# Norms of queries and keys by logarithm and exponential, their multiplication on GpSimd, and a new place for ScalarE's first squares

## The chip, the cores and the metric

One core of a Trainium2 chip runs the whole program. The metric is the device time of one execution in microseconds, as the median of several runs. Lower is better. The engines are TensorE (PE; PEld is its weight load), VectorE (DVE), ScalarE (ACT), GpSimd (POOL) and SyncE (SP), which issues DMAs. Each takes its own list of instructions in order, and they wait for each other by semaphores.

## What is computed

The reference is a sequence of four attention blocks and four feed-forward blocks on x of shape 8 x 512 x 128. The change lies in one of them, the local transformer with six layers, 16 heads of 64 and windows of 32 tokens. Its attention, cut to what matters here:

```
qkv = x @ Wqkv                        # 128 -> 3 x 1024
q, k, v = split(qkv), heads of 64
q = q / max(norm(q), 1e-12) * q_scale
k = k / max(norm(k), 1e-12) * k_scale
q = q * cos * scale + rotate_half(q) * sin * scale
k = k * cos / scale + rotate_half(k) * sin / scale
sim = q k^T * 8, in blocks of 32 queries by 64 keys, masked
out = softmax(sim) v
x = x + out @ Wo, then x + feed-forward with GELU, for each of six layers
```

The norm is a number per token and head. It can be multiplied in after the rotation, since the rotation is linear.

## The kernel before

The phase in question is `local_transformer_phase`. It takes the tokens of one sequence (512) as four tiles of 128, and so 6 layers x 8 sequences x 4 = 192 tiles; the text calls the four of a sequence tiles 0 to 3 (k % 4 in the code). Each engine runs one loop over k from -2 to 199 with the same stages in it, so that tile k is in its attention while the queries and keys of tile k + 1 are being finished and tile k + 2 is being projected. The order on each engine is the order of the calls in its loop; nothing else sorts them.

In iteration k, TensorE makes the scores of tile k (`make_scores`, L1205 and L1212), the values of k + 1 (`project_v`), the queries of k + 2 (`project_qk(.., 0)`, L1184 to L1186), turns the attention output of k - 1 (`turn_out`, L1273), makes the keys of k + 2 (`project_qk(.., 1)`), turns the probabilities of k (`turn_probs`, L1249), turns queries and then keys of k + 1 (`turn_qk`, L1262, eight transposes each), weighs the values of k in two halves (`weigh_values`, L1288) with the output projection of k - 1 between them (`project_out`, L1300), and does one step of the feed-forward block of an earlier sequence: `ffn_a` (L1338) in tile 0, `ffn_out` (L1343) and `ffn_turn` (L1316) in tile 1, `ffn_back` (L1323) in tile 2, `ffn_gate` (L1332) in tile 3.

Two waits of TensorE matter. The keys of tile k + 1 are turned into banks 4 and 5, which hold the projected queries of k + 2 until VectorE has read them; so `turn_qk(m, 1)` waits for `products_ready` of tile m + 1. And `project_out` writes bank 2, from which ScalarE copies the turned queries; so it waits for `qkt_copied`.

VectorE, in iteration k: `centre` (row maximum and subtraction of the scores, L1585 and L1588), `normalise` of queries and keys of k + 1 (L1595, rotated values times inverse norm), `products` of k + 2 (L1605, the projected values times cosines into `rot`, times sines into `sines`, for queries and then keys), `sum_squares` (L1610), in tile 2 `ffn_shift` (L1643), `divide` (L1616 and L1620), the second `sum_squares`, `add_output`, the second `divide`. In tile 1 the statistics of the feed-forward block come last (L1632 to L1639); they give `var_ready`.

`products(m, a)` waits for `squared` of the same tile, since ScalarE squares the same banks first. ScalarE, in iteration k: `copy_v` of k + 1 (L1413), `exponentials` of k (L1406), `square(k + 2, 0)` (L1418, queries), `copy_out` of k - 1 (L1435), `square(k + 2, 1)` (keys), `copy_probs` of k (L1423), `copy_qk` of k + 1 for queries and keys (L1430), and then the feed-forward step: `copy_turned` in tile 1, `ffn_normalise` (L1450) and `scale_norm` (L1457) in tile 2, `gelus` (L1464) in tile 3, with a table load before and after (L1460 and L1465). `ffn_normalise` waits for VectorE's shift, and `ffn_back` on TensorE for `ffn_normalise`.

GpSimd, in iteration k: in tile 2 `invert_deviation` (L1538, a power), `rotate` of k + 2 (L1526, four additions of 128x512 in place in `rot`), in tile 1 the low halves of the next sequence's tokens (L1516 and L1517), then `invert_norms` of k + 2 for queries and keys (L1532 guards the sum of squares from below, L1534 raises it to the power -1/2).

## Time and profile before

| | us |
|---|---|
| median of three runs | 4828.77 |
| lowest and highest run | 4828.52, 4838.41 |
| profiled execution, its own time | 4834.84 |
| its span | 4832.9 |
| TensorE busy (share) | 4224.5 (87%) |
| VectorE busy | 3624.7 (75%) |
| GpSimd busy | 2849.5 (59%) |
| ScalarE busy | 2545.3 (53%) |

The busy shares are an average over all phases of the program. A group row gives the busy time of one line, the mean of one instruction in ns, and then the idle time of its engine right before it with what ended that. A timeline row gives start and duration in us; where several equal instructions were merged, "x8" says how many, and the duration is that of all. In brackets stands the idle time of the engine before it and who ended it. Matmuls overlap, so starts are compared with starts.

### The profile page before, as it was taken

Reading aid. Unit: us, or ns where it says so; the run is one execution under the profiler, and the core shown is the slowest. Engines: PE = TensorE matmul, PEld = TensorE weight load, DVE = VectorE, ACT = ScalarE, POOL = GpSimd, SP = SyncE. Lnnn points to the kernel's source line nnn. Section 1 sums busy time; section 2 is a strip of 40 time slices with the busy share of each in tenths; the row PEclk is TensorE's granted clock in tenths of the full one; section 3 lists DMA queues with packets and bytes.
Section 4 is the critical chain, followed back from the end, with each engine's and each line's share of the span. In section 5 each row is a group of like instructions: output and inputs, shape, how many; then the busy total and the mean of one; then the engine's idle time right before and its main releaser. Section 6 shows DMA issues by size and latency. Waiting matters only on the chain. (4 is left out here: it accounts for less than half of the span.)

```text
span 4832.9 us, 167342 instructions
## 1 busy us (share of the span) xinstructions
PE 4224.5 (87%) x70890; PEld 3379.5 (70%) x70890; DVE 3624.7 (75%) x5894; ACT 2545.3 (53%) x3896; POOL 2849.5 (59%) x2141
## 2 busy tenths in 40 slices
PE   6997899999999999999999999999997749658667
PEld 5885677777777777777777777777775439548447
DVE  4445888888888888888888888888885564564554
ACT  2232456655566556565556565566654317546435
POOL 2223777777777777777777777777772037516025
PEclk9776999999999999999999999999998869868878
DMA  0001222232222322222222222222221021222022
GB/s 25 0 0 39 75 63 63 69 79 69 63 70 62 85 62 70 64 80 67 67 67 80 68 63 70 63 68 67 67 66 37 0 59 50 68 61 61 7 63 74
DMA packets 214198, 281.51 MB, mean 58 GB/s; under 512 B 58878, under 2 KB 103716, under 8 KB 212740
## 3 DMA queue, kind: packets, MB, share of 16 engines
q1 hardware_dynamic: 203972, 251.85, 20.1%
q0 software_dynamic: 9536, 19.55, 1.4%
q8 instruction: 545, 8.93, 0.8%
q14 instruction: 145, 1.19, 0.1%
HBM read 54.88 MB, written 18.28 MB: 15 GB/s over the span
## 5 line engine op out<-in xcount | busy, mean ns | idle before, releaser
L1526 POOL TENSOR_TENSOR local_rot<-local_rot,local_sines 128x512 f32<-128x512 f32 x768 | 955.2, 1278 | 825.1 <-DVE local_sines L1605 825.1
L1534 POOL TENSOR_TENSOR local_inv_norm<-local_norm2c,minus_half 128x16 f32<-128x16 f32 x384 | 1126.9, 2935 | 32.0
L1413 ACT COPY local_v_tile<-local_bank 128x1024 f32<-128x1024 f32 x192 | 195.0, 1016 | 713.0 <-PE local_bank L1186 702.6
L1184 PE MATMUL local_bank<-local_wqkv_hi,local_ys_hi 128*128 128x512 f32 x1152 | 491.3, 426 | 23.6 <-POOL local_ys_lo L1517 10.4
L1262 PE MATMUL local_bank<-ident,local_normed 128*128 128x128 f32 x3072 | 405.4, 275 | 91.0 <-DVE local_sines L1605 80.6
L1595 DVE TENSOR_TENSOR local_normed<-local_rot,local_inv_norm 128x1024 f32<-128x1024 f32 x384 | 455.3, 1218 | 32.9 <-issue 26.4
L1605 DVE TENSOR_TENSOR local_rot<-local_bank,local_table 128x1024 f32<-128x1024 f32 x384 | 467.7, 1218 | 7.0 <-issue 7.0
L1605 DVE TENSOR_TENSOR local_sines<-local_bank,local_table 128x1024 f32<-128x1024 f32 x384 | 467.3, 1217 | 0.0
L1610 DVE TENSOR_REDUCE local_norm<-local_squares 128x16 f32<-128x1024 f32 x384 | 464.7, 1211 | 0.0
L1186 PE MATMUL local_bank<-local_wqkv_hi,local_ys_lo 128*128 128x512 f32 x1152 | 453.8, 394 | 0.0
L1185 PE MATMUL local_bank<-local_wqkv_lo,local_ys_hi 128*128 128x512 f32 x1152 | 453.3, 394 | 0.0
L1585 DVE TENSOR_REDUCE local_top<-local_bank 128x16 f32<-128x1024 f32 x192 | 234.8, 1223 | 272.4 <-PE local_bank L1212 272.4
L1262 PEld LDWEIGHTS local_bank<-ident,local_normed 128*128 128x128 f32 x3072 | 339.9, 142 | 132.4 <-issue 120.5
L1300 PE MATMUL local_bank<-local_att_t,local_wo 128*128 128x128 f32 x3072 | 396.7, 283 | 1.6 <-ACT local_att_t L1435 1.3
L1418 ACT ACTIVATE local_squares<-local_bank 128x1024 f32<-128x1024 f32 x384 | 393.0, 1024 | 9.2 <-PE local_bank L1186 6.2
L1300 PEld LDWEIGHTS local_bank<-local_att_t,local_wo 128*128 128x128 f32 x3072 | 359.9, 193 | 20.0 <-ACT local_att_t L1435 1.5
L1288 PE MATMUL local_bank<-local_vals,local_probs_t 64*32 64x65 f32 x24576 | 336.7, 225 | 5.3 <-issue 3.0
L1212 PEld LDWEIGHTS local_bank<-local_k_t,local_q_t 64*32 64x32 f32 x24576 | 256.2, 105 | 104.7 <-issue 104.5
L1288 PEld LDWEIGHTS local_bank<-local_vals,local_probs_t 64*32 64x32 f32 x24576 | 270.3, 106 | 64.0 <-issue 39.6
L1212 PE MATMUL local_bank<-local_k_t,local_q_t 64*32 64x64 f32 x24576 | 289.8, 226 | 20.4 <-issue 20.4
L1620 DVE TENSOR_TENSOR local_att<-local_bank,local_inv_sum 128x512 f32<-128x512 f32 x384 | 265.5, 691 | 13.2
L1184 PEld LDWEIGHTS local_bank<-local_wqkv_hi,local_ys_hi 128*128 128x128 f32 x1152 | 217.6, 189 | 77.9 <-issue 25.7
...
## 6 DMA issues: line engine op xcount, KB each, us to landing
...
```

Source lines behind the costliest of these rows:

```text
L1184: nc.tensor.matmul(out, hi, wqkv_hi[:, d0:d1], start=True, stop=False)
L1185: nc.tensor.matmul(out, hi, wqkv_lo[:, d0:d1], start=False, stop=False)
L1186: return nc.tensor.matmul(out, lo, wqkv_hi[:, d0:d1], start=False, stop=True)
L1212: last = nc.tensor.matmul(bank[b * BLOCK:(b + 1) * BLOCK, SCORES[odd], c * WIN:(c + 1) * WIN], q_t[rows, c, b * BLOCK:(b + 1) * BLOCK], k_ ...
L1262: last = nc.tensor.transpose(bank[:, QK_TURN[a][j // 4], j % 4 * P:(j % 4 + 1) * P], normed[:, (8 * a + j) * P:(8 * a + j + 1) * P], g.ide ...
L1288: last = nc.tensor.matmul(bank[b * BLOCK:(b + 1) * BLOCK, WEIGHED[i][odd], j * (HD + 1):(j + 1) * (HD + 1)], probs_t[rows, c, b * BLOCK:(b ...
L1300: last = nc.tensor.matmul(bank[:, WO_BANK, 0:P], wo[:, c, :], att_t[:, c, :], start=(c == 0), stop=(c == CH - 1))
L1526: last = nc.gpsimd.tensor_tensor(of_heads(rot, a)[:, :, to], of_heads(rot, a)[:, :, to], of_heads(sines, a)[:, :, of], ALU.add)
L1534: nc.gpsimd.tensor_tensor(inv_norm[:, cols], norm2c[:, cols], g.minus_half[:, cols], ALU.pow).then_inc(q["inv_norms_ready"], 1)
L1595: nc.vector.tensor_tensor(of_heads(normed, a), of_heads(rot, a), inv_norm[:, a * HEADS:(a + 1) * HEADS].unsqueeze(2).to_broadcast([P, HEAD ...
L1605: last = nc.vector.tensor_tensor(of_heads(out, a), src, table[:, m % TILES, row, :].unsqueeze(1).to_broadcast([P, HEADS, HD]), ALU.mult)
L1610: nc.vector.tensor_reduce(norm2[:, cols], of_heads(squares, a), AX, ALU.add).then_inc(q["norms_ready"], 1)
```

## The change

Four things change, all in the local phase.

- The multiplication by the inverse norm (`normalise`) goes from VectorE to GpSimd. `rotate` now writes its sums into `normed`, and `normalise` multiplies `normed` in place. Since `normed` is what TensorE turns, `rotate` of a tile waits for `qk_turned` of the tile before, and `normalise` waits for the inverse norms.
- GpSimd's power is gone. It guards all 32 sums of squares in one instruction (`guard_norms`), and ScalarE makes the inverse norms as exp(-0.5 ln n) in two activations of 128x32, at the head of its iteration k for tile k + 1 (`invert_norms`).
- `square(k + 2, 0)` stands ahead of `exponentials(k)` instead of behind it.
- Both functions, and the exponential of the softmax, come from one table set that is loaded by name, once ahead of the loop and once after each sequence's gelus, there in place of a tiny exponential that had caused the load.

VectorE's `products(m, a)` now waits for `rotated` of tile m - 1, and `sum_squares` for `norms_guarded` of it.

```diff
+                def invert_norms(m):
+                    act.wait_ge(q["norms_guarded"], tile("norms_guarded", m))
+                    nc.scalar.activation(log_norm[:], norm2c[:], ACT.Ln).then_inc(q["logs_ready"], 1)
+                    act.wait_ge(q["logs_ready"], tile("logs_ready", m))
+                    act.wait_ge(q["qk_normed"], tile("qk_normed", m - 1))
+                    nc.scalar.activation(inv_norm[:], log_norm[:], ACT.Exp, scale=-0.5).then_inc(q["inv_norms_ready"], 1)
...
-                    nc.scalar.activation(table_pick[:, 2:3], table_pick[:, 0:1], ACT.Exp)
-
+                    nc.scalar.preload_act_table_set("natural_log_exp_and_others")
+
+                nc.scalar.preload_act_table_set("natural_log_exp_and_others")
...
                     if is_tile(k + 1):
+                        invert_norms(k + 1)
                         copy_v(k + 1)
+                    if is_tile(k + 2):
+                        square(k + 2, 0)
                     if is_tile(k):
                         exponentials(k)
-                    if is_tile(k + 2):
-                        square(k + 2, 0)
...
                     pool.wait_ge(q["products_ready"], tile("products_ready", m, a + 1))
+                    pool.wait_ge(q["qk_turned"], tile("qk_turned", m - 1, a + 1))
...
-                        last = nc.gpsimd.tensor_tensor(of_heads(rot, a)[:, :, to], of_heads(rot, a)[:, :, to], of_heads(sines, a)[:, :, of], ALU.add)
+                        last = nc.gpsimd.tensor_tensor(of_heads(normed, a)[:, :, to], of_heads(rot, a)[:, :, to], of_heads(sines, a)[:, :, of], ALU.add)
...
-                def invert_norms(m, a):
...
-                    nc.gpsimd.tensor_tensor(inv_norm[:, cols], norm2c[:, cols], g.minus_half[:, cols], ALU.pow).then_inc(q["inv_norms_ready"], 1)
+                def guard_norms(m):
+                    pool.wait_ge(q["norms_ready"], tile("norms_ready", m))
+                    nc.gpsimd.tensor_scalar(norm2c[:], norm2[:], 1e-24, None, ALU.max).then_inc(q["norms_guarded"], 1)
+
+                def normalise(m, a):
+                    pool.wait_ge(q["rotated"], tile("rotated", m, a + 1))
+                    pool.wait_ge(q["inv_norms_ready"], tile("inv_norms_ready", m))
+                    nc.gpsimd.tensor_tensor(of_heads(normed, a), of_heads(normed, a), inv_norm[:, a * HEADS:(a + 1) * HEADS].unsqueeze(2).to_broadcast([P, HEADS, HD]),
+                                            ALU.mult).then_inc(q["qk_normed"], 1)
...
+                    if is_tile(k + 1):
+                        normalise(k + 1, 0)
+                        normalise(k + 1, 1)
                     if is_tile(k + 2):
                         rotate(k + 2, 0)
                         rotate(k + 2, 1)
...
-                        invert_norms(k + 2, 0)
-                        invert_norms(k + 2, 1)
+                        guard_norms(k + 2)
...
-                    dve.wait_ge(q["qk_normed"], tile("qk_normed", m - 1, a + 1))
+                    dve.wait_ge(q["rotated"], tile("rotated", m - 1, a + 1))
...
-                    if is_tile(k + 1):
-                        normalise(k + 1, 0)
-                        normalise(k + 1, 1)
```

ScalarE's list in a tile 2, before, from the values to the keys:

```order
L1413 COPY local_v_tile<-local_bank 128x16x64
L1406 ACTIVATE local_scores<-local_scores 128x1024
L1418 ACTIVATE local_squares<-local_bank 128x1024
L1435 COPY local_att_t<-local_bank 128x1024
L1418 ACTIVATE local_squares<-local_bank 128x1024
L1423 COPY local_probs_t<-local_bank 128x1024
L1430 COPY local_q_t<-local_bank 128x1024
L1430 COPY local_k_t<-local_bank 128x8x128
```

The same place in the changed kernel (its line numbers are higher):

```order
L1436 ACTIVATE local_log_norm<-local_norm2c 128x32
L1439 ACTIVATE local_inv_norm<-local_log_norm 128x32
L1415 COPY local_v_tile<-local_bank 128x16x64
L1420 ACTIVATE local_squares<-local_bank 128x1024
L1408 ACTIVATE local_scores<-local_scores 128x1024
L1444 COPY local_att_t<-local_bank 128x1024
L1420 ACTIVATE local_squares<-local_bank 128x1024
L1425 COPY local_probs_t<-local_bank 128x1024
L1432 COPY local_q_t<-local_bank 128x1024
L1432 COPY local_k_t<-local_bank 128x8x128
```

The first squares and the exponentials have changed places, and the two small activations stand at the head.

GpSimd's list around a tile 2, before: the end of tile 1 (from the low halves on), the power for the deviation, and rotation and norms of tile 2:

```order
L1516 TENSOR_TENSOR local_ys_lo<-XH,local_ys_hi 64x512
L1517 TENSOR_TENSOR local_ys_lo<-XH,local_ys_hi 64x512
L1532 TENSOR_SCALAR local_norm2c<-local_norm 128x16
L1534 TENSOR_TENSOR local_inv_norm<-local_norm2c,minus_half 128x16
L1532 TENSOR_SCALAR local_norm2c<-local_norm 128x16
L1534 TENSOR_TENSOR local_inv_norm<-local_norm2c,minus_half 128x16
L1538 TENSOR_TENSOR local_rstd<-local_var_eps,minus_half 128x4
L1526 TENSOR_TENSOR local_rot<-local_rot,local_sines 128x16x32 x4
```

The same place in the changed kernel:

```order
L1527 TENSOR_TENSOR local_ys_lo<-XH,local_ys_hi 64x512
L1528 TENSOR_TENSOR local_ys_lo<-XH,local_ys_hi 64x512
L1543 TENSOR_SCALAR local_norm2c<-local_norm 128x32
L1553 TENSOR_TENSOR local_rstd<-local_var_eps,minus_half 128x4
L1548 TENSOR_TENSOR local_normed<-local_normed,local_inv_norm 128x1024 x2
L1538 TENSOR_TENSOR local_normed<-local_rot,local_sines 128x16x32 x4
```

The four instructions for the norms have become one, and the two multiplications stand between the deviation and the rotation of the tile after.

## Rows read from the trace of the kernel before

**Rows 1.** windows of the phase: stretch, length, busy time (count) by engine
```profile
510.00:3680.00 3170.00, 3008.07 (x63005) 2357.83 (x62989) 2764.74 (x3546) 1885.73 (x2278) 2299.29 (x1654) 1.00 0.27 69
```

**Rows 2.** waits of the whole span: who waited for whom, total us, times, longest
```profile
PE local_bank L1262 <- DVE local_sines L1605: 80.6, 185, 4.5
```

**Rows 3.** timeline of TensorE, tile 0: start, us, engine, line, operation, count [idle before]
```profile
2025.42 0.39 PE L1186 MATMUL local_bank<-local_wqkv_hi,local_ys_lo 128*128 128x512 f32 x1
...
2027.91 1.04 PE L1249 MATMUL local_bank<-ident,local_scores 128*128 128x128 f32 x8
2028.78 1.04 PE L1262 MATMUL local_bank<-ident,local_normed 128*128 128x128 f32 x8
2030.04 1.06 PE L1262 MATMUL local_bank<-ident,local_normed 128*128 128x128 f32 x8 [0.22 <-DVE local_sines L1605]
2031.04 0.86 PE L1288 MATMUL local_bank<-local_vals,local_probs_t 64*32 64x65 f32 x64
2031.83 2.05 PE L1300 MATMUL local_bank<-local_att_t,local_wo 128*128 128x128 f32 x16
```

**Rows 4.** timeline of ScalarE, the same tile
```profile
2025.39 1.06 ACT L1406 ACTIVATE local_scores<-local_scores 128x1024 f32<-128x1024 f32 x1
2026.36 1.01 ACT L1418 ACTIVATE local_squares<-local_bank 128x1024 f32<-128x1024 f32 x1
2027.27 1.00 ACT L1435 COPY local_att_t<-local_bank 128x1024 f32<-128x1024 f32 x1
2028.15 1.04 ACT L1418 ACTIVATE local_squares<-local_bank 128x1024 f32<-128x1024 f32 x1
2029.08 1.01 ACT L1423 COPY local_probs_t<-local_bank 128x1024 f32<-128x1024 f32 x1
2029.96 1.04 ACT L1430 COPY local_q_t<-local_bank 128x1024 f32<-128x1024 f32 x1
```

**Rows 5.** timeline of TensorE, tile 2 (the third) of the sequence before
```profile
1996.38 1.04 PE L1262 MATMUL local_bank<-ident,local_normed 128*128 128x128 f32 x8
1998.40 1.07 PE L1262 MATMUL local_bank<-ident,local_normed 128*128 128x128 f32 x8 [0.98 <-DVE local_sines L1605]
...
2003.92 0.63 PE L1323 MATMUL local_bank<-ident,local_y_hat 128*128 128x128 f32 x4 [0.89 <-ACT local_y_hat L1450]
```

**Rows 6.** timeline of VectorE, the same tile 2
```profile
1990.53 0.17 DVE L1639 TENSOR_SCALAR local_var_eps<-local_mean_var 128x4 f32<-128x4 f32 x1
...
1998.17 1.22 DVE L1605 TENSOR_TENSOR local_rot<-local_bank,local_table 128x1024 f32<-128x1024 f32 x1
...
2001.55 0.54 DVE L1643 SCALAR_TENSOR_TENSOR local_shift<-local_mean_var,local_rstd 128x4 f32<-128x4 f32 x1
```

**Rows 7.** timeline of ScalarE, the same tile 2
```profile
2002.12 1.65 ACT L1450 ACTIVATE local_y_hat<-local_y_tok,local_shift,local_rstd 128x128 f32<-128x128 f32 x4 [1.61 <-DVE local_shift L1643]
```

**Rows 8.** GpSimd's groups by form: line, names, shapes, count, busy us, mean ns
```profile
L1534 POOL TENSOR_TENSOR local_inv_norm<-local_norm2c,minus_half 128x16 f32<-128x16 f32 x384 | 1126.9, 2935 | 32.0
L1526 POOL TENSOR_TENSOR local_rot<-local_rot,local_sines 128x512 f32<-128x512 f32 x768 | 955.2, 1278 | 825.1 <-DVE local_sines L1605 825.1
...
L388 POOL TENSOR_SCALAR moe_row_of<-moe_at_col,moe_row_id 128x1136 bf16<-128x1136 bf16 x4 | 19.5, 4882 | 0.0
...
L387 POOL TENSOR_TENSOR moe_row_of<-moe_at_col,moe_row_id 128x1136 bf16<-128x1136 bf16 x4 | 12.9, 3235 | 38.4 <-DVE moe_at_col L520 38.4
...
L2023 POOL TENSOR_TENSOR delta_wkbd<-delta_wkb,delta_e_dec 128x512 f32<-128x512 f32 x8 | 8.4, 1046 | 0.0
```

**Rows 9.** ScalarE's groups by form, a very small one
```profile
L1977 ACT ACTIVATE delta_ln_u<-delta_e_u 128x4 f32<-128x4 f32 x8 | 1.6, 205 | 0.1
```

**Rows 10.** timeline of ScalarE, end of the tile 3 ahead of that tile 0
```profile
2021.73 1.28 ACT L1465 ACT_TABLE_LOAD   x1
```

**Rows 11.** timeline of GpSimd, filling of the phase
```profile
478.10 0.27 POOL L1532 TENSOR_SCALAR local_norm2c<-local_norm 128x16 f32<-128x16 f32 x1
```

**Rows 12.** timeline of TensorE, filling of the phase
```profile
489.23 1.94 PE L1262 MATMUL local_bank<-ident,local_normed 128*128 128x128 f32 x8 [4.50 <-DVE local_sines L1605]
```

21 lines of the change are left out of this document (7 added, 14 removed).

## The prediction

> **What bounds the kernel now.** I first cut the span by phases. The windows view shows that the local transformer phase takes 3,170 of 4,833 us from its second tile on, and that TensorE is busy for 3,008 of them at a granted clock of 1.00 (its upper level, 2.4 GHz), while VectorE has 2,765, GpSimd 2,299 and ScalarE 1,886 [rows 1]. So at most 162 us are to be had from waits of TensorE in this phase; relief of any other engine is worth only what it takes from them. The phase handles 192 tiles, four to a sequence; I call them tiles 0 to 3. The waits view then names the largest hole with a cause in another engine: before the turning of queries and keys (L1262) TensorE waits for VectorE's products of the next tile, 80.6 us in 185 times [rows 2]. The timelines say how they arise. In an ordinary tile the turning of queries starts at 2028.78 and that of keys at 2030.04, 1.26 us later, though its eight transposes need only what the turning of the probabilities takes ahead of it (2027.91 to 2028.78, 0.87 us) [rows 3]. The gap is therefore 0.39 us from start to start. In tile 2 it is 2.02 instead of 0.87 [rows 5], and there comes a second hole, 0.89 us in which TensorE waits for ScalarE's feed-forward rows at 2003.92 [rows 5].
>
> **The part taken from VectorE.** The two normalising multiplications (L1595), which stand ahead of the products, leave VectorE in each tile. That alone moves nothing: the products also wait for the squares, which ScalarE makes. Hence the new place of the first squares. I work through an ordinary tile by its rows. The last matmul of the query projection ends at 2025.42 + 0.39 = 2025.81 [rows 3], and ScalarE follows TensorE by 0.04, so the squares start at 2025.85. ScalarE's steps, from start to start, are 0.91 for squares, 0.97 for the exponentials, 0.88 for the copy of the turned output (2027.27 to 2028.15), 0.93 for the second squares and 0.88 for the probabilities [rows 4]. In the new order the squares end at 2026.9 (2027.4 before). The query products, freed of the normalising, take 2.3 us from 2026.9 and end at 2029.2, ahead of 2029.65, when TensorE could start on the keys. The wait for them goes.
>
> **What is late next.** The exponentials now start at 2026.76 and end at 2027.82; TensorE wants them at 2027.91 [rows 3], so this costs at most 0.1 if the signal takes long. The rest of ScalarE's chain: copy at 2027.73, second squares at 2028.61, probabilities at 2029.54 and ready at 2030.55, queries at 2030.42 and ready at 2031.46. The weighing (L1288) wants the probabilities; without its old delay it would start at 2031.04 - 0.39 = 2030.65. The output projection (L1300) writes the bank that the copy of the queries reads, so it can start at 2031.46 plus a signal. Signals from ScalarE to TensorE took 0.15 at the end of tile 2 (2002.12 + 1.65 = 2003.77, then 2003.92) [rows 5, 7]; the shortest that I grant is 0.05. The projection started at 2031.83 [rows 3]; it now starts at 2031.51 to 2031.61, a gain of 0.22 to 0.32. With the other delays of this chain (a late exponential moves nothing but the probabilities) I take 0.24. ScalarE has become as tight as TensorE: that is why I don't book the full 0.39. Tiles 0, 1 and 3 are 144: 144 x 0.24 = 34.6 us, with ends of 0 (each signal 0.15 slower than I think) and 144 x 0.39 = 56.
>
> **Tile 2.** It lies 32.40 us ahead of the ordinary one (1996.38 against 2028.78) [rows 3, 5], so its first squares start at 1993.45, the second at 1993.45 + 0.91 + 0.97 + 0.88 = 1996.21 and end at 1997.25. The key products start then; before, they started at 1998.17 [rows 6]. From there to the shift (L1643) it is two products and a sum of squares, as before: 2001.55 - 1998.17 = 3.38 [rows 6]. So the shift comes at 2000.67, 0.87 us sooner, ScalarE's rows (L1450) and TensorE's turning back with it. TensorE itself would be there yet sooner, so it still waits; what counts is the 0.87. In 48 sequences: 41.8 us, with ends of 30 (the shift gains two thirds) and 48 x 1.15 = 55 (the whole hole of the keys).
>
> **The new steps on ScalarE.** Two activations of 128x32 a tile. The smallest of this kind took 205 ns [rows 9]; with the wait between them I take 0.6 us. They stand ahead of the copy of the values, where ScalarE is idle: the copy waits for TensorE. In tile 0 this is narrow: the table load after the last gelu ends at 2021.73 + 1.28 = 2023.01 [rows 10], the norms are there at 2023.65, and the copy is due some 0.9 us ahead of the exponentials of 2025.39 [rows 4], at 2024.5. The code names one table set for logarithm and exponential, and the order of the changed kernel has no load between them; it has one more in all, ahead of the first weight split, where ScalarE sits idle anyway. I cost all this at nothing; its cover in tile 0 is 0.8 us.
>
> **The new steps on GpSimd.** Two multiplications of 128x1024 by a spread operand. The nearest row is L2023, the same operation on 128x512: 1046 ns, so 2.1 us each; by the additions of rotate it is 2 x 1278 = 2.56 [rows 8], and by the bfloat16 rows at the most 3235 x 1024 / 1136 = 2.9 [rows 8]. I take 2.1. GpSimd gives up two powers of 2.9 us a tile [rows 8] and gets some 4.2, so it isn't fuller. The question is when it is done. In tile 0 it starts at 2023.65 and ends the keys at 2027.9; TensorE wants them at 2029.65. In tile 2 it first waits for the variance (1990.53 + 0.17) [rows 6], makes its power of about 1.0 us, starts at 1991.8 and ends at 1996.0; wanted are the queries at 1996.38 and the keys at 1997.25. Both fit, with 1.7 and 1.2 us over. Tile 3 has its norms behind the feed-forward rows of ScalarE, by my working 7.1 us ahead of the keys' time, and tile 1 has yet more.
> The new wait of rotate for the turned queries and keys (it writes the buffer that TensorE reads) has the guard of the norms queued behind it: rotate starts at about 2029.9, as now, and the guard comes at 2035, long before the next tile's logarithm.
> On what GpSimd costs the page GPSIMD Engine Reference of the Trainium skill (3.1, Elementwise) speaks against the change: about 2.6 cycles an element with two inputs, twice VectorE's time. By that the price would be 2.2 us, an estimate from the page; the sum stays as it is, since this fits into the 3.0 that tile 0 leaves.
>
> **The fill.** For tile 0 of the phase the chain is bare. The guard ends at 478.37 [rows 11]; then came two powers and the normalising, and the keys were turned at 489.23 after a wait of 4.50 [rows 12]. Now: norms at 479.05, ScalarE's copy and squares to 481.1, query products to 483.4, GpSimd's keys at 483.3, keys turned at 483.5. That is 5.7 us once.
>
> **Sum.** 34.6 + 41.8 + 5.7 = 82.1 us. The profiled execution took 4834.84 us with a span of 4832.9; the median of the runs is 4828.77, 6 us lower, and the steps are the same in it. I take the sum from the median: 4746.7, so **4747 us**. Layer changes (five) are priced like their neighbours, though VectorE is the bound there and could give a little more.
>
> **Rivals.**
> *ScalarE eats the ordinary tiles.* Exponentials and probabilities come each 0.9 us later, and TensorE waits at L1249 or L1288 for what it saved at L1262. For it: the margins worked out above are 0.1 us. Against it: every step is from this trace. Tiles 0, 1, 3 then give nothing: 4828.8 - 47.5 = 4781.
> *TensorE alone bounds.* The chain of ScalarE is a little faster than I add up: 0.39 in each of 144 tiles, 0.87 in 48, 5.7 and some 6 at layer changes: 4828.8 - 110 = 4719.
> *GpSimd becomes late, slower than before.* Gelus, table load, logarithm, exponential and two slow multiplications are one chain in tile 0; variance, power and the same two in tile 2. At p us each, the keys are late by 2p - 6.0 in tile 0 (2023.65 + 2p against 2029.65) and by 2p - 5.5 in tile 2. A sequence gains 1.7 us, so it turns at 4p - 11.5 = 1.7, p = 3.3. The nearest row on that side is the two-step GpSimd operation at 4.88 us for 1136 elements, 4.4 for 1024 [rows 8]. At p = 4, with 0.9 in tile 3, it is 5.4 us a sequence on top of 4747: about 5005. Against it stand two rows of 2.1 and 2.6.
> *Nothing comes of it.* Another wait of the same size stands at the same place, say the keys' bank still waits for products: 4829.
>
> **How the numbers follow.** My forecast has a chance of 0.70 (4730 to 4765), the eaten tiles 0.11, TensorE alone 0.08, GpSimd late 0.07, nothing 0.04. A range of 4712 to 4790 takes the first three. About 0.2% is what a measurement of this kernel can tell from no change: faster 0.89, same 0.04, slower 0.07.
>
> **What would show it.** Right: the line "PE L1262 waits for VectorE's sines" gone or under 10 us in all; ordinary tiles of about 16.2 us from L1205 to L1205 instead of 16.45; tile 2 about 15.1; the shift row 0.9 sooner after the turned queries; GpSimd's multiplication at 2.0 to 2.6 us; ScalarE and GpSimd named nowhere before L1262. Wrong: waits of TensorE for the exponentials (L1249) or the probabilities (L1288) of over 0.2 us a tile; waits at L1262 for GpSimd; table loads beside the pairs around the gelus; a VectorE that runs slower while GpSimd multiplies.

## The result and the profile after

The changed kernel takes **4804.4 us** (median of four runs, 4800.65 to 4813.37) against 4829.24 us for the kernel before in the same set: a ratio of 0.9947, 95% interval 0.9928 to 0.9966. It is faster, by 25 us. Forecast were 82 us and a range of 4712 to 4790, so the time lies outside the range. In microseconds at 4829 the interval means 17 to 35 us less. The profiled execution took 4813.37 us with a span of 4811.3.

The windows view of the phase, changed kernel (stretch, length, busy time and count of PE, PEld, VectorE, ScalarE, GpSimd, then granted clock, DMA share, GB/s); it answers [rows 1]:

```profile
510.00:3680.00 3170.00, 3033.77 (x63121) 2367.06 (x63119) 2395.78 (x3172) 1948.63 (x2617) 1868.62 (x1462) 0.99 0.26 68
```

VectorE lost 369 us of work and GpSimd 431. TensorE gained only 26 in an equal stretch of time, and its clock is no longer 1.00 on the mean.

TensorE's waits inside the phase, from 500 to 3640 (who waited for whom, total us, times, longest), first before, then after:

```profile
PE local_bank L1262 <- DVE local_sines L1605: 75.9, 183, 3.7
PE local_bank L1323 <- ACT local_y_hat L1450: 39.0, 44, 0.9
PE local_bank L1212 <- issue: 19.5, 14, 1.9
PE local_bank L1184 <- issue: 7.0, 5, 1.4
...
PE local_bank L1288 <- issue: 3.0, 6, 0.9
```

```profile
PE local_bank L1325 <- ACT local_y_hat L1459: 47.7, 46, 1.5
PE local_bank L1214 <- issue: 32.3, 24, 1.9
PE local_bank L1290 <- issue: 23.9, 59, 1.7
PE local_bank L1186 <- issue: 15.4, 5, 3.1
```

The wait of [rows 2] at the turned queries and keys is gone: L1264 (L1262 before) is not in the list. But 76 us of waits went and 25 came off the time. "issue" means that TensorE stood still and the profile names no other engine. I call these the unnamed gaps; the entries shown grew from 29.5 to 71.6 us (19.5 + 7.0 + 3.0, then 32.3 + 23.9 + 15.4).

TensorE in tile 0 of a sequence, changed kernel; it answers [rows 3]:

```profile
2012.94 1.05 PE L1251 MATMUL local_bank<-ident,local_scores 128*128 128x128 f32 x8
2013.89 1.94 PE L1264 MATMUL local_bank<-ident,local_normed 128*128 128x128 f32 x16
2015.76 0.86 PE L1290 MATMUL local_bank<-local_vals,local_probs_t 64*32 64x65 f32 x64
2016.63 2.02 PE L1302 MATMUL local_bank<-local_att_t,local_wo 128*128 128x128 f32 x16
```

All sixteen transposes are one row now. From the probabilities' transposes to the output projection it is 3.69 us, 3.92 before (2031.83 - 2027.91, [rows 3]): the forecast's step for ordinary tiles, 0.24, is there to 0.01.

The same for tile 2, with VectorE's shift; it answers [rows 5, 6]:

```profile
1981.88 1.94 PE L1264 MATMUL local_bank<-ident,local_normed 128*128 128x128 f32 x16
...
1986.59 0.34 PE L1290 MATMUL local_bank<-local_vals,local_probs_t 64*32 64x65 f32 x14
1987.34 0.73 PE L1290 MATMUL local_bank<-local_vals,local_probs_t 64*32 64x65 f32 x50 [0.41 <-issue]
1988.69 0.63 PE L1325 MATMUL local_bank<-ident,local_y_hat 128*128 128x128 f32 x4 [0.62 <-ACT local_y_hat L1459]
```

```profile
1986.10 0.76 DVE L1654 SCALAR_TENSOR_TENSOR local_shift<-local_mean_var,local_rstd 128x4 f32<-128x4 f32 x1
```

The shift comes 4.22 us after the first turned queries, 5.17 before; but it takes 0.76 instead of 0.54, and the rows of the feed-forward are turned back 6.81 us after them instead of 7.54. So 0.73 is left of the 0.87.

What was added cost about what the forecast said: GpSimd's multiplication from the page's groups (mean 1926 ns), ScalarE's two activations from the views of their lines (least, median, largest ns):

```profile
L1548 POOL TENSOR_TENSOR local_normed<-local_normed,local_inv_norm 128x1024 f32<-128x1024 f32 x384 | 731.6, 1926 | 326.3 <-ACT local_inv_norm L1439 326.3
```

```profile
L1436 ACT ACTIVATE local_log_norm<-local_norm2c x192: 217/229/245, 479.4 to 3641.5; 128x32 f32<-128x32 f32 x192
L1439 ACT ACTIVATE local_inv_norm<-local_log_norm x192: 229/229/232, 479.6 to 3641.8; 128x32 f32<-128x32 f32 x192
```

**Where the time went.** I took TensorE's timeline of 46 sequences (all but the first and the last) and measured each stretch from its first start to the first start of the next kind. This is the ledger, with means of one sequence (four tiles) in us:

| stretch | before | after | difference |
|---|---|---|---|
| turned queries and keys (L1264) | 9.70 | 7.47 | -2.23 |
| turned probabilities (L1251) | 3.60 | 3.72 | +0.12 |
| first half of the weighing (L1290) | 3.17 | 3.50 | +0.33 |
| output projection (L1302) | 7.97 | 7.84 | -0.13 |
| second half, with tile 2's wait for ScalarE's rows | 4.25 | 5.13 | +0.88 |
| scores (L1214) | 6.21 | 6.52 | +0.31 |
| projections and turned output (L1186, L1275) | 20.88 | 21.35 | +0.47 |
| feed-forward products and band | 10.99 | 10.99 | 0 |
| sum | 66.77 | 66.51 | -0.26 |

46 x 0.26 = 12 us. The first scores came 5.2 us sooner (492.27 before, 487.06 after), and the remaining sequences and the end hold the last 4 of the 21.6 us between the two spans. Of 2.23 us that a sequence gained, 1.97 came back in other places. Some of that the forecast had taken off already (it booked 0.24 of 0.39 in an ordinary tile, and 0.87 of 1.15 in tile 2). The first half of the weighing is such a case: it isn't slower. In the changed kernel the output projection starts 0.14 us after the end of ScalarE's copy of the turned queries in all four kinds of tile (medians), in the kernel before 0.7 to 1.4 us after it; so TensorE now waits there for ScalarE, as the forecast had it, in a pause too short for the wait list. The experiments are about the other places: the projections (five layer changes), the second half of the weighing (the shift, and gaps), the scores (gaps).

### The profile page after: what moved, and what is told of

It reads as the page before. It is cut to its first block and busy times, and to the rows that moved or that the text cites. A ratio compares the mean times of both kernels' runs of the same rounds, so it can differ in the third digit from the quotient of the medians.

```text
span 4811.3 us, 167679 instructions
## 1 busy us (share of the span) xinstructions
PE 4235.1 (88%) x70890; PEld 3379.2 (70%) x70890; DVE 3249.3 (68%) x5510; ACT 2605.4 (54%) x4233; POOL 2417.1 (50%) x1949
## 3 DMA queue, kind: packets, MB, share of 16 engines
q8 instruction: 545, 8.93, 0.8%
## 5 line engine op out<-in xcount | busy, mean ns | idle before, releaser
L1538 POOL TENSOR_TENSOR local_normed<-local_rot,local_sines 128x512 f32<-128x512 f32 x768 | 953.5, 1276 | 788.6 <-PE local_bank L1264 784.0
L1548 POOL TENSOR_TENSOR local_normed<-local_normed,local_inv_norm 128x1024 f32<-128x1024 f32 x384 | 731.6, 1926 | 326.3 <-ACT local_inv_norm L1439 326.3
L1186 PE MATMUL local_bank<-local_wqkv_hi,local_ys_hi 128*128 128x512 f32 x1152 | 496.2, 431 | 31.6 <-issue 15.4
L1615 DVE TENSOR_TENSOR local_sines<-local_bank,local_table 128x1024 f32<-128x1024 f32 x384 | 466.5, 1215 | 0.0
L1302 PE MATMUL local_bank<-local_att_t,local_wo 128*128 128x128 f32 x3072 | 390.4, 280 | 4.4 <-ACT local_att_t L1444 1.2
L1302 PEld LDWEIGHTS local_bank<-local_att_t,local_wo 128*128 128x128 f32 x3072 | 358.7, 192 | 30.3 <-issue 12.9
L1264 PE MATMUL local_bank<-ident,local_normed 128*128 128x128 f32 x3072 | 373.6, 275 | 4.7 <-POOL local_normed L1548 4.1
L1290 PE MATMUL local_bank<-local_vals,local_probs_t 64*32 64x65 f32 x24576 | 348.8, 225 | 26.4 <-issue 23.9
L1264 PEld LDWEIGHTS local_bank<-ident,local_normed 128*128 128x128 f32 x3072 | 333.8, 142 | 23.9 <-POOL local_normed L1548 5.4
L1290 PEld LDWEIGHTS local_bank<-local_vals,local_probs_t 64*32 64x32 f32 x24576 | 273.7, 105 | 94.0 <-issue 69.7
L1214 PEld LDWEIGHTS local_bank<-local_k_t,local_q_t 64*32 64x32 f32 x24576 | 256.2, 105 | 118.9 <-issue 118.9
L1214 PE MATMUL local_bank<-local_k_t,local_q_t 64*32 64x64 f32 x24576 | 291.4, 225 | 33.3 <-issue 33.1
L1186 PEld LDWEIGHTS local_bank<-local_wqkv_hi,local_ys_hi 128*128 128x128 f32 x1152 | 220.2, 191 | 86.0 <-issue 33.9
L1188 PEld LDWEIGHTS local_bank<-local_wqkv_hi,local_ys_lo 128*128 128x128 f32 x1152 | 219.9, 191 | 50.9
```

Of the source, the lines that this page charges most:

```text
L1186: nc.tensor.matmul(out, hi, wqkv_hi[:, d0:d1], start=True, stop=False)
L1188: return nc.tensor.matmul(out, lo, wqkv_hi[:, d0:d1], start=False, stop=True)
L1214: last = nc.tensor.matmul(bank[b * BLOCK:(b + 1) * BLOCK, SCORES[odd], c * WIN:(c + 1) * WIN], q_t[rows, c, b * BLOCK:(b + 1) * BLOCK], k_ ...
L1264: last = nc.tensor.transpose(bank[:, QK_TURN[a][j // 4], j % 4 * P:(j % 4 + 1) * P], normed[:, (8 * a + j) * P:(8 * a + j + 1) * P], g.ide ...
L1290: last = nc.tensor.matmul(bank[b * BLOCK:(b + 1) * BLOCK, WEIGHED[i][odd], j * (HD + 1):(j + 1) * (HD + 1)], probs_t[rows, c, b * BLOCK:(b ...
L1302: last = nc.tensor.matmul(bank[:, WO_BANK, 0:P], wo[:, c, :], att_t[:, c, :], start=(c == 0), stop=(c == CH - 1))
```

## The experiments

Two theories stood at the start. **LOCK**: VectorE's operations with two inputs in SBUF and GpSimd's now longer and otherwise placed operations slow each other; that is the loss at the layer changes and at the shift. **FETCH**: the "issue" gaps are TensorE waiting for its own instructions, and they grow since the waits that used to hide this are gone. The rival to both was that ScalarE's new order (the squares ahead of the exponentials) moved the losses there. The edits are to the changed kernel unless another is named. The runs were made in sets, each with the kernel before in it, whose median lay between 4828 and 4836 us. Where a difference between two kernels of different sets is small, I give it twice, by the medians and by the ratios to the kernel before (in us at 4829).

### The layer changes

The three engines around the layer change at 2042, changed kernel:

```profile
2042.83 5.76 DVE L1596 TENSOR_TENSOR local_wqkv_lo<-local_stage,local_wqkv_hi 128x1024 fp32r<-128x1024 f32 x2
```

```profile
2042.64 4.87 POOL L1548 TENSOR_TENSOR local_normed<-local_normed,local_inv_norm 128x1024 f32<-128x1024 f32 x2
```

```profile
2045.85 0.76 PE L1186 MATMUL local_bank<-local_wqkv_hi,local_ys_hi 128*128 128x512 f32 x1 [3.09 <-issue]
```

VectorE splits two thirds of the new layer's weights while GpSimd multiplies. TensorE needs the first split: it ended at 2045.75, and TensorE went on at 2045.85. So this hole is a wait for VectorE, though the profile calls it "issue", and it belongs to LOCK, not to FETCH. Least, median and largest ns of the split, before (L1579) and after (L1596):

```profile
L1579 DVE TENSOR_TENSOR local_wqkv_lo<-local_stage,local_wqkv_hi x18: 1211/1224/1237, 460.1 to 3145.8; 128x1024 fp32r<-128x1024 f32 x18
```

```profile
L1596 DVE TENSOR_TENSOR local_wqkv_lo<-local_stage,local_wqkv_hi x18: 1221/2918/2921, 461.4 to 3131.3; 128x1024 fp32r<-128x1024 f32 x18
```

**e1_yield**: GpSimd waits at the layer changes until both splits are made.

```diff
                     if is_tile(k + 1):
+                        if (k + 2) % PER_LAYER == 0 and k > 0 and is_tile(k + 2):
+                            pool.wait_ge(split_lo, 3 * ((k + 2) // PER_LAYER) + 2)
                         normalise(k + 1, 0)
```

> The changed kernel, but at a layer change GpSimd waits with its two multiplications until VectorE has split the first two parts of the new weights. In the changed kernel the two splits took 5.76 us beside the multiplications (2.35 before the change) and tile 2 of a layer change 21.2 us (19.1 before). Theory LOCK (a VectorE instruction with two inputs in SBUF and a GpSimd instruction hold each other up): splits back at 2.3 us, multiplications at 3.8 for two instead of 4.87, tile 2 of the five layer changes at about 18.4, so 5 x 2.9 = 14 us less than the changed kernel (about 4790), and no fall of the granted clock at the layer changes. Rival WEIGHTS LATE (the splits wait for the loaded weights or for ScalarE's cast, which now come later relative to TensorE): splits stay near 5.8 us, time as the changed kernel, 4804, or a little above.

Measured: 4792.03 us (six runs), ratio 0.991 (0.9894 to 0.9926), under the changed kernel by 12 us by the medians and by 18 by the ratios. By the ledger it is 17: 0.38 us in each of 46 sequences, nearly all of it in tile 2, where a layer change takes 17.8 us instead of 21.3. The split and TensorE's wait:

```profile
L1598 DVE TENSOR_TENSOR local_wqkv_lo<-local_stage,local_wqkv_hi x18: 1212/1215/1225, 460.9 to 3112.2; 128x1024 fp32r<-128x1024 f32 x18
```

```profile
PE local_bank L1186 <- issue: 6.9, 5, 1.4
```

Windows of 20 us over the same layer change, after and with the wait, which has it 6 us sooner (the third number from the right is the granted clock):

```profile
2040.00:2060.00 20.00, 14.68 (x313) 12.05 (x291) 19.18 (x29) 11.46 (x16) 10.94 (x7) 0.91 0.18 48
```

```profile
2034.00:2054.00 20.00, 15.85 (x456) 13.07 (x456) 17.65 (x32) 13.81 (x21) 10.43 (x9) 1.00 0.19 49
```

The splits are back at 1215 ns, the long hole of 3.1 us is 1.4 again, and the clock, which had fallen to the lower of its two levels (1.2 of 2.4 GHz) for 3.4 to 6.8 us behind each of these holes, stays at the upper one. The rival, that the splits wait for weights that come late, is out: it forecast splits of nearly 5.8 us for two. LOCK holds here: an operation with two SBUF inputs took 2.9 us instead of 1.2 beside GpSimd, and GpSimd's, which overlapped it, up to 2.88 us instead of 1.90. The Trainium skill says of the port pair that the two engines share ("SBUF — State Buffer", the section on the two separate sides) that it is an exclusive lock which the first of the two holds for its whole instruction. The trace agrees to about 0.1 us if they take turns by whole operations. At 2042.64 GpSimd's first multiplication starts; alone it takes 1.90, so it would end at 2044.54. The split that starts at 2042.83 ends at 2045.75, which is 2044.54 and its own 1.21. The second multiplication ends at 2047.51, against 2045.75 + 1.90 = 2047.65, and the second split at 2048.59, against 2047.51 + 1.21 = 2048.72. The products of VectorE, with one input in PSUM, took 1.22 us as before beside the same multiplications. **e4_multiply_on_vector**, further down, is a second test: with nothing of GpSimd's beside them the splits took 1.21 us and tile 2 of a layer change 19.1, as before the change.

### The shift

**e3_shift_on_gpsimd**: the four numbers per row of the shift are worked out by GpSimd right behind its power; VectorE only makes the negated mean, earlier.

```diff
+                    nc.vector.tensor_scalar(neg_mean[:], mean_var[:, :, 0], -1.0, None, ALU.mult)
...
-                    nc.vector.scalar_tensor_tensor(shift[:], mean_var[:, :, 0], -1.0, rstd[:], ALU.mult, ALU.mult).then_inc(q["shift_ready"], 1)
...
+                    pool.wait_ge(q["rstd_ready"], seq("rstd_ready", n))
+                    nc.gpsimd.tensor_tensor(shift[:], neg_mean[:], rstd[:], ALU.mult).then_inc(q["shift_ready"], 1)
```

> The changed kernel, but the shift (minus mean times inverse deviation) is made by GpSimd right after its power, 14 us ahead, instead of by VectorE behind the sums of squares, where it took 0.76 us (0.54 before the change, 0.16 when alone). Theory: the wait of TensorE before the turning back of the feed-forward rows (about 1.0 us in each of 46 tiles 2) hangs on VectorE's list; now ScalarE makes the rows right behind the copy of the keys, 1.5 us sooner, the wait goes, and tile 2 falls from 15.30 to about 14.4: 48 x 0.9 = 43 us less than the changed kernel, 4762, minus what stalls of TensorE without a cause in another engine take back. Rival SUPPLY (TensorE's own instruction stream stalls, a constant of the program): tile 2 falls but tile 3 grows by as much, 4795 to 4804.

Measured: 4757.84 us (4752.35 to 4760.55), ratio 0.9839 (0.9826 to 0.9851): 47 us less than the changed kernel by the medians, 52 by the ratios, and so about twice what the whole change gave. The shift's line and what TensorE then waits for:

```profile
L1556 POOL TENSOR_TENSOR local_shift<-local_neg_mean,local_rstd x48: 201/203/233, 575.9 to 3633.0; 128x4 f32<-128x4 f32 x48
```

```profile
PE local_bank L1215 <- issue: 36.2, 33, 2.2
PE local_bank L1291 <- issue: 21.1, 51, 1.2
```

The wait for ScalarE's rows, 47.7 us in 46 times, is gone. It never was a matter of arithmetic: 0.2 us of work stood in VectorE's list behind 3.4 us of products. Not all of the gain is the shift's. At a layer change GpSimd's multiplications now stand behind the shift, and start 0.1 us after the first split instead of 0.2 us ahead of it: it took 1.21 us in all five, only the second 2.92, and tile 2 of a layer change fell to 18.3 to 19.8 us.

**e10_before_shift** does the same to the kernel before, and nothing else.

> The kernel before, with one part of e3_shift_on_gpsimd alone: the shift is worked out by GpSimd behind its power, and VectorE makes the negated mean only; nothing else is changed. The wait of the feed-forward's copies for y_hat is 0.89 us in the 44 tiles that have it, 39 us. If that goes and TensorE starts its next products as before, 4790. If TensorE's own gaps ahead of the scores in the next tile take a third of it back, as in the changed kernel, 4803. If the wait goes to something else in the same place, 4829 stays.

Measured: 4819.33 us, ratio 0.9968 (0.9957 to 0.9978). That is 10 us by the medians of the two sets, 16 by the ratio, less than the 26 or 39 expected. Its two largest waits:

```profile
PE local_bank L1263 <- DVE local_sines L1608: 93.5, 184, 4.2
PE local_bank L1213 <- issue: 23.6, 27, 1.7
```

By the ledger, tile 2 fell from 16.33 to 15.44 us and tile 3 rose from 17.00 to 17.50; of that 0.50, 0.36 is a longer wait for VectorE's products and 0.17 the scores. In the kernel before VectorE was the next to be late, in the changed one it is not: by the ratios the shift is worth 16 us there and 52 here. So the change is worth more than its own time shows.

**e6_yield_shift** has both edits, e1's and e3's.

> The two edits of e1 and e3 together: GpSimd waits at layer changes until VectorE has split two parts of the weights, and GpSimd makes the shift. If the two are independent, the gains over the changed kernel add up: 48 us of e3 and 12 to 17 of e1, so about 4743 and a ratio of 0.981 to the kernel before. If the same slack is counted twice (a layer change's tile 2 has both), 4750.

Measured: 4741.09 us (4735.64 to 4755.75), ratio 0.9824 (0.9804 to 0.9843), the fastest of all by its median. The sum of the two gains had forecast about 4743, the rival (the same slack counted twice) 4750, a ratio of 0.984. The interval holds both, so the time doesn't decide between them. The trace shows what the wait adds to e3: both splits are at 1.21 to 1.23 us, and tile 2 of a layer change takes 16.6 to 16.8 us.

### Order and place of the work

**e2_old_order** puts the exponentials ahead of the first squares again, **e7_yield_shift_old** does that to e6.

```diff
-                    if is_tile(k + 2):
-                        square(k + 2, 0)
                     if is_tile(k):
                         exponentials(k)
+                    if is_tile(k + 2):
+                        square(k + 2, 0)
```

> The changed kernel with the exponentials again ahead of the first squares; all else stays. Theory of the prediction (the wait at L1262 goes because the squares are earlier): products of the queries end at about 29.65 instead of 29.2 on the clock of rows 3, just when TensorE wants them; ScalarE's chain of six starts 0.46 us earlier, since it need not idle for the query projection. Ordinary tiles 16.15 to 16.25 as in the changed kernel (16.20), time within 8 us of it. Rival ORDER CARRIES IT: the wait at L1262 comes back with some 0.25 us a tile, 144 x 0.25 = 36 us slower than the changed kernel, 4840.

> The kernel of e6_yield_shift (GpSimd waits at layer changes, shift on GpSimd) with the exponentials again ahead of the first squares on ScalarE. If the place of the squares is worth nothing here too, as in e2_old_order, the time is that of e6_yield_shift, 4741 us within 8. If the old order spares TensorE the short gaps behind the weighing products (4.7 us over 15 in e2_old_order against 23.9 over 59), up to 15 us less, 4726. If ScalarE now delays the value products or the queries' normalising, since the shift is gone and less time stands in tile 2, up to 10 us more.

Measured: 4807.1 us, ratio 0.9946 (0.9933 to 0.996), the same as the changed kernel; and 4755.84 us, ratio 0.9841 (0.9825 to 0.9857). That is 15 us over e6 by the medians, 8 by the ratios, and the two intervals overlap. The new place of the squares is worth nothing that is sure to show in the time. Three waits of e2:

```profile
PE local_bank L1214 <- issue: 30.3, 24, 1.9
...
PE local_bank L1264 <- DVE local_sines L1615: 10.8, 47, 0.5
...
PE local_bank L1290 <- issue: 4.7, 15, 1.5
```

A named wait of 10.8 us is back, and the unnamed one behind it fell from 23.9 to 4.7. This is an exchange, and e7 shows the same one (13.8 and 4.1). In undisturbed ordinary tiles e2 takes 16.31 us, against 16.45 before and 16.20 in the changed kernel. So 0.14 of the 0.25 come from freeing VectorE alone, without the new place of the squares, where the forecast said that this "alone moves nothing".

**e4_multiply_on_vector** gives the multiplications back to VectorE; logarithm, exponential and the new order stay.

```diff
-                    nc.gpsimd.tensor_tensor(of_heads(normed, a), of_heads(normed, a), inv_norm[:, a * HEADS:(a + 1) * HEADS].unsqueeze(2).to_broadcast([P, HEADS, HD]),
+                    nc.vector.tensor_tensor(of_heads(normed, a), of_heads(rot, a), inv_norm[:, a * HEADS:(a + 1) * HEADS].unsqueeze(2).to_broadcast([P, HEADS, HD]),
```

> The changed kernel with the multiplication by the inverse norms back on VectorE, behind the centring, from rot into normed as before; logarithm and exponential on ScalarE and the new place of the squares stay. Theory: the move carries the gain. Products of the queries start at 27.55 again, so TensorE waits 0.39 at L1262: ordinary tiles 16.45; tile 2 at 15.9; about 4823 (the fill keeps a few us). If inverse norms on ScalarE alone had carried it, 4805. Layer changes near 19 us, since GpSimd then has nothing beside the splits (LOCK); 21 by WEIGHTS LATE.

Measured: 4819.19 us, ratio 0.9964 (0.9951 to 0.9976), where 4823 was expected. Tile 2 keeps its gain (median 15.32 us against 15.96 before and 15.30 after) and the ordinary tiles lose theirs (undisturbed 16.45 us, as before, against 16.20). So tile 2 owed its gain to the replaced power, for which VectorE's second multiplication used to wait (the power ended at 1994.67), and the ordinary tiles to the move to GpSimd. The forecast had put both down to the freed VectorE. The wait, in the kernel before:

```profile
1994.76 1.23 DVE L1595 TENSOR_TENSOR local_normed<-local_rot,local_inv_norm 128x1024 f32<-128x1024 f32 x1 [0.54 <-issue]
```

### What makes the unnamed gaps

**e5_nops** was to shift TensorE's stream of instructions once, by 128.

```diff
+                for _ in range(128):
+                    pe.nop()
                 for k in range(-2, ALL + 8):
```

> The changed kernel with 128 no-ops in TensorE's list right ahead of the loop of the local phase, where TensorE waits anyway; every later instruction stays, but lies 128 places further in the instruction stream. Question: what the gaps of TensorE are for which the profile names no cause ('issue': 32 us before the scores, L1214, most of them in tiles 3, and 24 us at L1290). Theory FETCH (TensorE's instructions come in by pieces of fixed size, and it runs dry in dense stretches of small matmuls where a piece ends): the gaps move to other tiles of a sequence (tile 3's median falls from 17.1 towards 16.2 and another's rises), sum within 15 us of the changed kernel. Rival WAIT (a semaphore or DMA that the profile does not name): the gaps stay in tiles 3 before the scores, each within 0.2 us.

Measured: 4802.35 us, ratio 0.9934 (0.9915 to 0.9953), and the same gaps (31.3 us in 22 at the scores). I first read that as the end of the idea that gaps come at piece ends of the stream. It was no test: the gaps stood after the same numbers of records as in the changed kernel, and the queue that brings instructions moved as much, as the page's queue rows show (after, then e5: packets, MB, share). The no-ops never moved the places at which the gaps come.

```profile
q8 instruction: 545, 8.93, 0.8%
```

```profile
q8 instruction: 545, 8.93, 0.7%
```

**e8_half_scores** leaves out the score products of the odd heads.

```diff
-                            for odd in range(2):
+                            for odd in range(1):
```

> The changed kernel without the score products of every second head (64 of 128 small matmuls of make_scores in each tile are left out, with their weight loads; the scores of these heads are only the mask). Theory FETCH: gaps without a named cause before the scores (L1214) fall from 32 us to under 8, since the densest stretch of instructions is half as long; those at L1290 fall too. Rival WAIT: both stay at 20 us or more. The time itself falls by up to 0.7 us a tile, some 100 us, less where ScalarE's chain binds.

**e9_no_window_dma** leaves out the DMAs of the value windows from the ninth tile on.

```diff
+                    if m >= 8:
+                        for b in range(BLOCKS):
+                            sp.nop().then_inc(vals_loaded[p], 16)
+                        continue
```

> The changed kernel without the DMAs that spread the values over the windows, from the ninth tile of the phase on (the weighing reads what the first tiles left). They are 86% of the bytes that the DMA engines move in this phase. Question: is TensorE's instruction supply slowed by them? Rival TRAFFIC: gaps without a named cause at L1214 and L1290 fall from 56 us to under 20, and the time by about 40, to 4765. Theory FETCH by itself (piece size and pace of the stream, not traffic): gaps stay at 40 us or more, time 4795 to 4804.

Measured: 4699.86 us (one run) and 4790.38 us (ratio 0.9918, 0.9901 to 0.9934). In e8 no gap is left at the scores; 16.7 us in 44 times stay at the weighing. In e9 the scores' gaps stay and those of the weighing fall to a third:

```profile
PE local_bank L1221 <- issue: 33.2, 25, 1.9
...
PE local_bank L1297 <- issue: 8.5, 26, 0.7
```

Both kernels compute something else, which is why only their times and gaps are used. So it matters how dense the small products stand. e9 fits neither expectation (4765 and 4795 to 4804): the scores' gaps don't depend on the windows' traffic, and why those of the weighing fell is open. The packets that bring instructions were hardly quicker without it (median 0.99 us instead of 1.03 in the phase).

**e11_band_cover** is e6 with the two band products of tile 3 written four times over, so that six wide products stand ahead of the scores there too.

```diff
-                    for odd in range(2):
+                    for odd in (0, 1) * (4 if t == 3 else 1):
                         nc.tensor.matmul(bank[:, SCORES[odd], :], ident16[:], band8[:, min(t, 1)].rearrange("p h k -> p (h k)"),
```

> The kernel of e6_yield_shift (4741 us, TensorE's gaps without a named cause ahead of the scores 34.6 us, nearly all in tile 3) with the two band products of tile 3 written four times over instead of once: six more products of 512 columns stand ahead of the scores, as six feed-forward products do in the other tiles, and write the same values again. In e6 the pair of band products takes 0.53 us, so the six more are worth 1.4 to 1.6 us per sequence, 67 to 77 us. If wide products ahead of the dense stretch let TensorE's supply of instructions catch up, the 34.6 us go nearly to nothing and the time is 4741 + 72 - 33 = 4780. If the gaps belong to something else that happens in tile 3, they stay and the time is 4813.

Measured: 4769.49 us, ratio 0.9869 (0.9854 to 0.9884). 1.29 us of work per sequence (the band's stretch went from 0.53 to 1.82) cost 0.51 (tile 3 from 17.38 to 17.89); the rest stood in place of gaps, which fell from 34.6 us (30 times) to what the row below shows. The six products also move the places, but at like places the gaps are shorter too: after 99 to 107 of the records explained below, e11 has 0.35 to 0.44 us (four gaps), and e6 1.35 to 1.37 (five gaps).

```profile
PE local_bank L1215 <- issue: 5.8, 11, 1.6
```

**e12_values_first** tried to have this for nothing: in e6, tile 3's value projections ahead of its scores.

```diff
+                    early = t == 3 and is_tile(k) and is_tile(k + 1)
+                    if early:
+                        project_v(k + 1, k)
                     if is_tile(k):
                         make_scores(k)
-                    if is_tile(k + 1):
+                    if is_tile(k + 1) and not early:
                         project_v(k + 1, k)
```

> The kernel of e6_yield_shift with the next tile's six value products put ahead of the scores in tile 3 alone; all other orders stay. No work is added. If wide products ahead of the scores close the gaps in front of them (34.6 us, some 0.65 us per sequence) and the exponentials, which now begin 1.4 us later in that tile, still end before their transposes, 4741 - 31 = 4710. If the exponentials are then late for the transposes, the 0.65 us come back there: 4741. If the gaps have another cause they stay, and the exponentials may add to them: 4741 to 4780.

Measured: 4756.08 us (4740.37 to 4760.95), ratio 0.9843 (0.983 to 0.9857), no better than e6. Its waits:

```profile
PE local_bank L1187 <- issue: 16.6, 29, 1.5
PE local_bank L1187 <- DVE local_wqkv_lo L1604: 15.8, 5, 3.2
PE local_bank L1215 <- issue: 10.1, 20, 1.4
```

The scores' gaps fell by 24 us, 9 of them came back ahead of the projections behind the scores, and 12 at the layer changes, where the values' weights are not split yet.

**The law in the positions.** A timeline row breaks where there is a gap, and its count says after how many matmul records. Each small product of the scores, of the weighing and of the padding in e13 and e14 is two such records (64 products of the scores make 128), and "after 127" below counts records. The scores of tile 3 in the changed kernel, in the sequences numbered 25 and 27 (from 0, of 48):

```profile
2193.16 1.47 PE L1214 MATMUL local_bank<-local_k_t,local_q_t 64*32 64x64 f32 x127
...
2196.30 0.24 PE L1214 MATMUL local_bank<-local_k_t,local_q_t 64*32 64x64 f32 x1 [1.68 <-issue]
...
2325.31 1.43 PE L1214 MATMUL local_bank<-local_k_t,local_q_t 64*32 64x64 f32 x122
...
2328.19 0.31 PE L1214 MATMUL local_bank<-local_k_t,local_q_t 64*32 64x64 f32 x6 [1.45 <-issue]
```

After 127, then 122, and on in steps of five or six each second sequence (117, 111, 106, 101, 96). A record is two instructions, a weight load and a matmul, so the place moves by ten or twelve in two sequences. If the stream is cut into pieces of 256 and a sequence is 133 over a whole number of pieces, two sequences are 266, ten over. I laid this over all unnamed gaps inside scores and weighing, with one free offset for each of the eight places in a sequence where gaps come: 80 of 84 gaps of the changed kernel lie within eight instructions of it, 74 of 78 of e6. In e11, which has twelve instructions more per sequence, 60 of 62 fit 145 = 133 + 12 and only 14 fit 133; a step at random fits some 16 to 19. e8 leaves out 512 instructions per sequence, two whole pieces, and all its 44 gaps fit 133. The queue rows say the same: 8.93 MB in 545 packets, about 16.4 KB each.

**The fetches themselves.** The trace holds the packets of this queue with their times. I set them beside the gaps. In the changed kernel TensorE goes on 1.20 to 1.61 us after such a packet has landed (median 1.40) in all 84 gaps, and 2.2 to 2.9 us after it started. For the gap after 127 records above: the packet started at 2193.60, landed at 2194.72, and TensorE went on at 2196.30; it had run out at 2194.62. It is the same in the kernel before (21 of 21 gaps), in e5 (71 of 71), e11 (62 of 62) and e14 (118 of 118). A moment taken evenly from the phase lies 1.15 to 1.65 us behind a landing in 8% of cases; of TensorE's 64 named waits 4 end there, and of the five holes at the layer changes none. So TensorE waits for its own instructions, and a gap is as long as the fetch is late. What sets off a fetch, and so why it is late, the runs don't show.

**e13_pad_bad** and **e14_pad_good** test it forward. Both put 31 small products (62 records, 124 instructions) in tile 2, ahead of the wait for ScalarE's rows; they make a sequence a whole number of pieces, nearly, so that the piece ends stay where they are. The second has 40 products more, once (160 instructions).

```diff
                     after_qk(k)
+                    for i in range((31 + (40 if n == 0 else 0)) * is_tile(k + 2)):
+                        rows, b = slice(HD * (i % 2), HD * (i % 2) + HD), i // 2 % BLOCKS
+                        nc.tensor.matmul(bank[b * BLOCK:(b + 1) * BLOCK, FFN_BACK + i % 2, 0:BLOCK], g.ident[rows, 0:BLOCK], g.ident[rows, 0:BLOCK], start=True, stop=True,
+                                         tile_position=(HD * (i % 2), b * BLOCK))
```

> The changed kernel with 31 small products (64 rows, 32 columns, into banks that are written over straight afterwards) ahead of TensorE's wait for the feed-forward's copy in tile 2, where it idles 1.04 us on the mean. Read from the traces: the short gaps of TensorE ahead of and inside the scores (L1214) and the weighing (L1290) always fall after the same number of instructions, if that number is counted in pieces of 256 and a sequence is 133 over a whole number of pieces (in the kernel with twelve instructions more per sequence, 145 over). 31 products are 124 instructions, so a sequence is now 257, one over, and the piece ends at nearly the same place in each sequence: in tile 3 after product record 127 to 104 of the scores. If a gap arises where a piece of the instruction stream ends deep in the dense scores, it now arises in nearly all 48 sequences instead of 24: gaps of 60 to 70 us ahead of L1214 instead of 32. The time is then 4804 + 33 = 4837, and up to 20 us more if the 31 products last longer than the wait. If the gaps are tied to the place in the work alone and not to the stream, the 32 us stay: 4804 to 4824.

> The same 31 products per sequence, and 40 more once, in the first sequence: 160 instructions, which move the end of the pieces in tile 3 to record 47 to 24 of the scores, where the traces show few gaps (none in the changed kernel). The work per sequence is the same as in the run before. If the stream decides, the gaps ahead of L1214 fall from 32 us to 10 or less, against 60 to 70 in the run before, and this kernel is some 50 to 65 us faster than that one, at about 4780. Gaps at the second weighing (L1290) then stand in tile 3 in nearly all sequences, 0.2 to 0.4 us each, and sum to 15 to 25 us. If the place of the piece ends is nothing, both kernels take the same time.

Measured: 4853.41 us (4850.94 to 4859.6), ratio 1.0046 (1.0032 to 1.006), and 4815.68 us (4813.45 to 4819.04), ratio 0.9965 (0.9952 to 0.9979). The two have the same work in every sequence but the first, and differ by 38 us. In the wait lists the first has 21 us more at the scores, 9 ahead of the projections, 9 ahead of the band and the output projection, and 19 more in the named wait for ScalarE's rows, but 18 less at the weighing. The last two are one exchange: in the second kernel TensorE stands still in the weighing of tile 2, and then has less to wait for right behind it. The waits at the scores, and one gap of each:

```profile
PE local_bank L1214 <- issue: 61.1, 43, 2.2
```

```profile
PE local_bank L1214 <- issue: 40.0, 49, 1.6
```

```profile
1747.93 1.47 PE L1214 MATMUL local_bank<-local_k_t,local_q_t 64*32 64x64 f32 x126
...
1751.04 0.27 PE L1214 MATMUL local_bank<-local_k_t,local_q_t 64*32 64x64 f32 x2 [1.65 <-issue]
```

```profile
1726.55 0.71 PE L1214 MATMUL local_bank<-local_k_t,local_q_t 64*32 64x64 f32 x46
...
1728.14 1.04 PE L1214 MATMUL local_bank<-local_k_t,local_q_t 64*32 64x64 f32 x82 [0.89 <-issue]
```

The first has a gap in the scores of tile 3 in every sequence from the ninth to the forty-seventh, and the 61.1 us forecast as 60 to 70. Each layer has eight sequences: the gaps stand after 127 records in the second layer, after 126, 125, 124 in the next three and after 123 in the last. In the first layer they stand one record further, ahead of the projection behind the scores (six gaps of 1.2 to 2.1 us). The second has them after 48 records in the first layer and 43 in the last. So the place is fixed to the instruction, and moves by one record at a layer change. (It was expected to drift by half a record per sequence, to 104 and 24; a sequence is 256 over a whole number and not 257. I take it that the first added product carries a wait that used to be an instruction of its own; that was not tested.) Its gaps didn't vanish: 40 us instead of at most 10. In the changed kernel a piece end at that place made no gap; with 62 records more in the same dense stretch it makes one of 0.8 us. So both matter, where the piece ends and how much time the work of the pieces before it takes; e14 shows the first and misjudged the second, and it stays over the changed kernel by 9 to 11 us instead of falling to 4780. FETCH holds: TensorE stands still at ends of 256-instruction pieces of its own stream, until 1.2 to 1.6 us after a fetch has landed. The Trainium skill describes such pieces ("Runtime: NRT & Kernel Launch", Instruction fetch mechanics): blocks of 256 instructions, fetched by the sequencer through a DMA queue of its own, at a cost that it calls mostly hidden. The pieces agree with the trace here (positions, and packets of 16384 bytes); the cost does not, since these gaps sum to 56 us in the changed kernel (32.3 + 23.9).

## Why the prediction failed, step by step

- **Wait at the keys, ordinary tiles (34.6 us).** Size right, and the route right with one step too many: 0.23 us between the named rows against 0.24, and undisturbed tiles of 16.20 us instead of 16.45, where 16.2 was forecast. The margins of 0.1 us on ScalarE held; it is named in waits of 1.7 us in all at L1251, and its copy of the queries holds the output projection, as forecast. What was wrong is that the freed VectorE "alone moves nothing": e2 has 0.14 of the 0.25 us without the new place of the squares.
- **Tile 2 (41.8 us).** The route was right, one term was mis-sized. The shift came 0.95 sooner, but took 0.76 us; the forecast carried over the 0.54 of [rows 6], a row that already held a lock (156 ns at the least), and didn't ask what GpSimd would do beside it. 0.73 of 0.87 is left between the rows, 0.67 in the median of the tile: 0.20 x 48 = about 10 us. It also put the gain down to the freed VectorE, where e4 shows it to be the replaced power.
- **Fill (5.7 us).** 5.2 in the one profiled execution of each kernel; the first scores of e1, e2, e3, e5 and e6, which have the same fill, came at 483.9 to 487.6, so the size is known to some 4 us only.
- **GpSimd and ScalarE.** 1.93 us instead of 2.1 and 0.23 per activation: hidden, as forecast. GpSimd was late nowhere in the steady state. The forecast had the interference on its list of signs ("a VectorE that runs slower while GpSimd multiplies"), but no price for it and no rival with it.
- **Layer changes "priced like their neighbours".** This step failed. VectorE's two-input splits now stand beside GpSimd's multiplications. e1 shows the price by undoing it alone: 12 us by the medians, 17 by the ledger, 18 by the ratios. Tile 2 of a layer change grew from 19.1 to 21.3 us where the forecast's own 0.87 would have given 18.2.
- **What was not in the sum.** TensorE's own supply, a term put at nothing without a reason, and the largest. The forecast took each wait as an amount that can be removed, with a start that moves up by as much. The unnamed gaps grew by 42 us in all between the two wait lists, 8 of them at the layer changes (the splits) and 34 at scores and weighing. At the scores and the weighing each ends 1.2 to 1.6 us behind the landing of a fetch, in both kernels. e2 and e4 show the exchange at the weighing: where a named wait at the keys is back, 4.7 and 5.9 us of unnamed gaps stand there instead of 23.9. At the scores they stay at 30.3 and 32.5. That such gaps existed stood in the trace of before (19.5 us at the scores), and no step asked about them. No rival had this.

82 - 10 (shift) - 12 to 18 (layer changes) - 34 (gaps) = 20 to 26 us; measured are 25 by the medians, and 22 between the spans of the two profiled executions. The terms come from different views and some of them exchange with each other, so the closeness is partly luck. The last is the largest, and is shown by positions, by the times of the fetches, and by two kernels that differ, but for 40 products in the first sequence, only in the place of the piece ends. What stays open: what sets off a fetch, and in part why the gaps at the scores grew from 14 to 24 in number. It isn't the wait at the keys of ordinary tiles, since e4 has it back and 25 gaps. It fits that tile 2, which stands right ahead of these scores, is shorter in both; e10, which shortens it in the kernel before and does nothing else, has 27.
